# A transformer block: gates and part of the first inner layer as fills, and steps of the attention loop ordered in twos

## The reference, cut to what matters

```python
def _mole(x, W, b, A, Bm, Rw):
    gates = jax.nn.softmax(jnp.einsum('bsd,de->bse', x, Rw), axis=-1)
    base = jnp.einsum('bsd,dh->bsh', x, W) + b
    z = jnp.einsum('bsd,edr->ebsr', x, A)
    zg = z * jnp.transpose(gates, (2, 0, 1))[..., None]
    return base + SCALING * jnp.einsum('ebsr,erh->bsh', zg, Bm)

h = _layernorm(x) * (1 + ca) + sa
x = x + ga * attention(h, W_qkv, b_qkv, W_out, b_out)
h = _layernorm(x) * (1 + cb) + sb
h = relu(_mole(h, W1, b1, A1, B1, R1))
x = x + gb * _mole(h, W2, b2, A2, B2, R2)
```

## Time and profile before

| what | us |
|---|---|
| median of 3 executions (lowest, highest) | 1315.23 (1310.58, 1323.12) |
| the profiled execution | 1316.99 |
| its span, first to last instruction | 1315.0 |
| PE busy | 1222.3 |
| DVE busy | 934.4 |
| ACT busy | 800.2 |
| POOL busy | 183.3 |

### The profile page before, as it was taken

One profiled execution on the slowest core, in us unless ns is written; L12 is line 12 of the kernel. 1 busy time (PEld: TensorE's weight loads), 2 busy tenths in 40 slices (PEclk: granted clock), 3 DMA queues, 4 the chain that ended last, 5 costly groups with the idle time before them and its releaser, 6 DMA issues.

```text
span 1315.0 us, 23664 instructions
## 1 busy us (share of the span) xinstructions
PE 1222.3 (93%) x9456; PEld 709.5 (54%) x9456; DVE 934.4 (71%) x1247; ACT 800.2 (61%) x1611; POOL 183.3 (14%) x153
## 2 busy tenths in 40 slices
PE   7988789999999999999999999999989999999997
PEld 6765333444444344444444444334334888888886
DVE  4877897888787888777888778776531477776653
ACT  4441466777667777767777767776664455454442
POOL 5205600000112000000000000201010133232310
PEclk9997799999999999999999989999787999999998
DMA  5793120031142022022022013400000122211100
GB/s 169 245 289 140 51 64 10 16 83 29 35 107 60 9 64 54 10 62 71 10 54 56 10 32 102 113 1 9 11 10 22 45 64 65 54 50 38 53 17 33
DMA packets 58118, 79.53 MB, mean 60 GB/s; under 512 B 12680, under 2 KB 28752, under 8 KB 58008
## 3 DMA queue, kind: packets, MB, share of 16 engines
q1 hardware_dynamic: 58008, 78.01, 20.3%
HBM read 47.57 MB, written 29.62 MB: 59 GB/s over the span
## 4 chain that ended last, share of the span: by engine, by line
PE 68%; DVE 17%; ACT 8%; issue 4%; SPq 2%; DMA 2%; ACTq 0%; DVEq 0%
PE ps L893 21%; PE ps L875 17%; PE ps L855 9%; PE ps L965 7%; PE ps L391 6%; ACT prob L1074 6%; PE ps L811 6%; DVE mx L1222 5%; DVE hid_lo L1365 4%; DVE xhat L419 1%; DVE stats L409 1%; SPq L453 1%; DMA xs<-in_x 1%; ACT o_sb L1059 1%; DVE x L1270 1%
## 5 line engine op out<-in xcount | busy, mean ns | idle before, releaser
L1074 ACT ACTIVATE prob<-ps 128x512 f32<-128x512 f32 (+3 forms) x1280 | 597.8, 536 | 267.9 <-PE ps L811 137.9
L1222 DVE TENSOR_REDUCE mx<-ps 128x2 f32<-128x1024 f32 (+1 forms) x512 | 591.5, 1187 | 164.1 <-PE ps L855 92.9
L875 PE MATMUL ps<-qst,kst 64*128 64x512 f32 (+3 forms) x1280 | 379.5, 450 | 14.9 <-ACT prob L1074 9.1
L875 PEld LDWEIGHTS ps<-qst,kst 64*128 64x128 f32 x1280 | 174.8, 188 | 325.9 <-ACT prob L1074 284.0
L893 PE MATMUL ps<-prob,vw 128*32 128x512 f32 (+3 forms) x2560 | 309.6, 557 | 9.2 <-ACT o_sb L1059 9.1
L855 PE MATMUL ps<-kst,qst 62*128 62x512 f32 (+3 forms) x1280 | 248.8, 419 | 23.3 <-DVE mx L1222 19.1
L855 PEld LDWEIGHTS ps<-kst,qst 62*128 62x128 f32 x1280 | 125.9, 193 | 68.6 <-DVE mx L1222 58.8
L811 PE MATMUL ps<-mask_kh,eye_h 64*128 64x128 bf16 x1024 | 100.8, 227 | 0.0
L893 PEld LDWEIGHTS ps<-prob,vw 128*32 128x32 f32 x2560 | 51.9, 109 | 74.9 <-ACT prob L1074 49.8
L1365 DVE TENSOR_TENSOR hid_lo<-hidf,hid_hi 128x512 fp32r<-128x512 f32 x64 | 73.1, 1182 | 13.8 <-ACT hid_hi L1114 13.7
L1218 DVE TENSOR_REDUCE mx<-ps 128x4 f32<-128x512 f32 x64 | 59.8, 954 | 21.1 <-PE ps L811 21.1
(11 more groups left out here) (157 smaller groups left out, 1358.0 us busy)
## 6 DMA issues: line engine op xcount, KB each, us to landing
qk_parts<-parts SPq DMA_DIRECT2D x32, 512.0 KB, 4.9
qst<-qk_parts SPq DMA_DIRECT2D x192, 64.0 KB, 2.4
kst<-qk_parts SPq DMA_DIRECT2D x192, 64.0 KB, 2.4
xs<-in_x SPq DMA_DIRECT2D x16, 512.0 KB, 8.4
o_all<-o_sb SPq DMA_DIRECT2D x32, 256.0 KB
o_raw<-o_all SPq DMA_DIRECT2D x16, 256.0 KB
rd<-rden_rows SPq DMA_DIRECT2D x16, 256.0 KB
out<-y SPq DMA_DIRECT2D x8, 512.0 KB, 3.2
```

The source lines that it names most:

```text
L875: last = pe.matmul(ps[:, banks[par], 0:BLK - skip], kst[g % 2][rows, pair, t * P:(t + 1) * P], qst[g % 2][rows, pair, J * BLK + skip:(J + ...
L1074: act.activation(prob[:, n % P_BUFS, h, 0:width], ps[:, L_BANK + i % L_BUFS, 0:width], ACT.Exp).then_inc(exp_done, 1)
L1222: dve.tensor_reduce(mx[:, u % 2, :, pairs[0], r, cb], ps[:, bank:bank + 2, 0:width], AX, ALU.max).then_inc(max_red, 1)
```

## The change

**Order of the steps.** Steps are taken in twos. A pair whose steps are off the diagonal, which is not the first pair of its unit, and which has at most four pieces of fills, goes a new way: values products come later, the first of them in two halves of its columns, and head 3 of the first step is paired with head 0 of the second. Other pairs keep the former order. Long fills are made in pieces (`pieces_of`): the projection and the routing in four, the turn and a hidden chunk in two.

**More of block 0 among the fills.** The front events get fixed steps: projection 285, scaling 290, turn 292, routing 295, weighing 297, gates 299, hidden chunks 0 to 3 at 302, 306, 310 and 314 (before, the projection was at 287, the turn at 302). They are inserted after the planner has placed the others. The maxima around them move by a step or two. ACT reads a hidden chunk in the step after it, in two halves behind heads 1 and 3. Chunks 4 and 5 stand before the last two values products. Then come the projection of block 1, chunks 6 and 7, and block 0's down products.

**Other places.** POOL casts and splits block 1's attention output behind the projection. The gate rows are computed after the first block's projections to q and k. The arrays of the last stage lie elsewhere: hidden chunk 2 of block 0 is in `o_raw` of even blocks, chunk 3 in `rd` of even blocks, and the load of block 2 has a wait for `z2_done`.

```diff
+EARLY_H = 4
+FRONT = [(285, ("project", 0)), (290, ("rescale", 0)), (292, ("turn_x", 0)), (295, ("route", 0)), (297, ("weigh", 0)),
+         (299, ("gates", 0))] + [(302 + 4 * m, ("hidden", m)) for m in range(EARLY_H)]
...
+ROOT_FRONT, GATE_FRONT = SLOT_OF[FRONT_FILL["project", 0]] + 3, SLOT_OF[FRONT_FILL["route", 0]] + 1
+def pieces_of(es):
+    parts = {"project": TT, "route": TT, "turn_x": KC, "hidden": KC}
+    return [(e, k) for e in es for k in range(parts.get(EVENTS[FILLS[e]][0], 1))]
...
+        for m, at in ((2, o_raw_at), (3, rd_at)):
+            hid_front.append(Region(at).pair(f"hid_{m}", [P, BLK]))
...
                 def load(i):
                     until(sp, o_lo, i - 1)
+                    if i == 2:
+                        sp.wait_ge(z2_done, 1)
...
-                load(2)
                 for q in range(2):
                     sp.wait_ge(o_stored[q], 16 * O_DMAS * NU // 2)
                     sp.wait_ge(rden_stored[q], 16 * NG // 2)
+                load(2)
...
                 normalise_o(1)
+                pool.wait_ge(o_norm, 2)
+                pool.wait_ge(fill_done, FRONT_FILL["project", 0] + 1)
+                pool.tensor_copy(oT[0][:], o_raw[1][:]).then_inc(o_hi, 1)
+                pool.wait_ge(o_hi, 2)
+                pool.tensor_tensor(oT[1][:], o_raw[1][:], oT[0][:].bitcast(F32), ALU.subtract).then_inc(o_lo, 1)
...
-                pe.wait_ge(setup, 2 * KC)
-                gate_rows()
                 pe.wait_ge(w_lo, 2)
                 project_qk(0, range(0, KC))
                 turn(1)
                 project_qk(0, range(KC, 2 * KC))
+                pe.wait_ge(setup, 2 * KC)
+                gate_rows()
...
+                    if ev[0] == "hidden":
+                        m = ev[1]
+                        pe.wait_ge(max_red, FRONT_FILL["gates", 0] + 1)
+                        pe.wait_ge(ffn_lo, 2 * W_PIECES)
+                        product(pe, ps[:, bank, :], lambda v, c: w1_p[v][:, k, m * P:(m + 1) * P],
+                                lambda v, c: hT2[0][v][:, k, :], 1, start=(k == 0), stop=False)
+                        if k == KC - 1:
+                            pe.matmul(ps[:, bank, :], bl1_s[:, m * P:(m + 1) * P], zgT_front[:],
+                                      start=False, stop=True).then_inc(fill_done, 1)
...
-                for n in range(NS):
-                    if n >= PV_LAG:
-                        values(n - PV_LAG)
-                    logits(n, 0)
-                    for e in ORDER[1 + n][:2]:
-                        fill(e)
-                    logits(n, 1)
-                    for e in ORDER[1 + n][2:]:
-                        fill(e)
-                for n in range(NS - PV_LAG, NS):
-                    values(n)
+                for n in range(0, NS, 2):
+                    each = [pieces_of(ORDER[1 + n]), pieces_of(ORDER[2 + n])]
+                    both = each[0] + each[1]
+                    u = STEPS[n][0]
+                    if not diagonal(n) and n > FIRST[u] and len(both) <= 4:
+                        logits((n, 0), (n, 1))
+                        for piece in both[0:1]:
+                            fill(*piece)
+                        logits((n, 2))
+                        values(n - 2, 0)
+                        logits((n, 3), (n + 1, 0))
+                        for piece in both[1:2]:
+                            fill(*piece)
+                        values(n - 2, 1)
+                        logits((n + 1, 1))
+                        for piece in both[2:3]:
+                            fill(*piece)
+                        logits((n + 1, 2), (n + 1, 3))
+                        values(n - 1)
+                        for piece in both[3:]:
+                            fill(*piece)
+                    else:
+                        for m in (n, n + 1):
+                            mine = each[m - n]
+                            cut = 1 if m + 1 in HIDDEN_STEP else 2
+                            if m >= PV_LAG:
+                                values(m - PV_LAG)
+                            logits((m, 0), (m, 1))
+                            for piece in mine[:cut]:
+                                fill(*piece)
+                            logits((m, 2), (m, 3))
+                            for piece in mine[cut:]:
+                                fill(*piece)
+                hidden_front(EARLY_H)
+                values(NS - 2)
+                hidden_front(EARLY_H + 1)
+                values(NS - 1)
...
-                pe.wait_ge(small_lo, 4)
-                pe.wait_ge(ffn_lo, 2 * W_PIECES)
-                route_in(0)
+                project_out(1)
+                for m in range(EARLY_H + 2, FC):
+                    hidden(0, m)
+                    hidden_low_rank(0, m)
...
+                def early_hidden_out(m, part):
+                    e = FRONT_FILL["hidden", m]
+                    act.wait_ge(fill_done, e + 1)
+                    if part == 0:
+                        if m >= 2:
+                            act.wait_ge(max_red, FRONT_FILL["hidden", m - 2] + 1)
+                        if m == 0:
+                            act.wait_ge(pv_done, LAST_OF_G[NG - 2] + 1)
+                    dst = hidf_front[:, m % 2, :] if part == 0 else hid_at(0, m, 0)
+                    act.activation(dst, ps[:, S_BANK + 2 * (e % 2), :], ACT.Relu,
+                                   bias=b1_sb[:, m:m + 1]).then_inc(f1_out, 1)
...
-                exponentials(0, z1_sub, z1_exp)
                 for i in range(NBLK):
                     if i >= 1:
-                        exponentials(i - 1, z2_sub, z2_exp)
-                    if i + 1 < NBLK:
+                        exponentials(i - 1, z2_sub, z2_exp, 1)
+                    if 1 <= i < NBLK - 1:
                         o_high(i + 1)
-                    gated_in(i)
-                    for m in range(FC):
+                    if i >= 1:
+                        gated_in(i)
+                    for m in range(0 if i >= 1 else EARLY_H, FC):
                         hidden_out(i, m)
```

More of the change, by code:

```diff
@@ L860, in fill, with routed, hidden_front, logits @@
                         for at in range(len(pairs)):
-                            last = mask((bank, bank + 1), (at + 1) * width - P, mask_qh)
+                            last = mask_queries(bank, (at + 1) * width - P)
                     last.then_inc(fill_done, 1)
-                def logits(n, pair):
+                def routed(i, bank, t):
+                    return product(pe, ps[:, bank, t * 32:t * 32 + ZP],
+                                   lambda v, k: hT2[i % 2][v][:, k, t * P:(t + 1) * P],
+                                   lambda v, k: ar1_p[v][:, k, :], KC)
+                def hidden_front(m):
+                    pe.wait_ge(max_red, NF)
+                    product(pe, ps[:, H_BANK + m % 2, :], lambda v, k: w1_p[v][:, k, m * P:(m + 1) * P],
+                            lambda v, k: hT2[0][v][:, k, :], KC, stop=False)
+                    pe.matmul(ps[:, H_BANK + m % 2, :], bl1_s[:, m * P:(m + 1) * P], zgT_front[:],
+                              start=False, stop=True).then_inc(f1_done, 1)
+                def logits(*heads):
+                    for n, h in heads:
+                        u, t = STEPS[n]
+                        g, J = UNITS[u]
+                        skip = skip_of(n)
+                        if n == FIRST[u] and h == 0:
+                            pe.wait_ge(m_in[u % 2], 16 * M_DMAS * (u // 2 + 1))
+                        until(pe, exp_done, 4 * n + h - L_BUFS + 1)
+                        rows = slice(h % 2 * STACK, h % 2 * STACK + ROWS + MROWS)
+                        last = pe.matmul(ps[:, L_BANK + (4 * n + h) % L_BUFS, 0:BLK - skip],
+                                         kst[g % 2][rows, h // 2, t * P:(t + 1) * P],
+                                         qst[g % 2][rows, h // 2, J * BLK + skip:(J + 1) * BLK],
+                                         start=True, stop=True)
+                        if not diagonal(n):
+                            last.then_inc(st_done, 1)
+                    if diagonal(heads[0][0]):
+                        mask_keys(heads)
+                def values(n, part=None):
                     u, t = STEPS[n]
@@ L1043, in _ @@
                 root(1)
-                act.wait_ge(rows_done, 1)
-                for v in range(2):
-                    act.copy(gates[:, v].rearrange("p b d -> p (b d)"), ps[:, V_BANK + v, :]).then_inc(rows_out, 1)
                 act.wait_ge(setup, 2 * KC + 1)
@@ L1393, in _ @@
                         gate_y(i - 1)
-                    if front:
+                    if front and back:
                         low_o(i + 1)
```

320 lines of the change are left out of this document (203 added, 117 removed).

## The result

| | us |
|---|---|
| before, median of 4 (lowest, highest) | 1316.43 (1310.58, 1323.12) |
| after, median of 4 (lowest, highest) | 1339.16 (1333.98, 1343.97) |
| ratio, 95% interval | 1.0178 (1.0139 to 1.0218) |
| the profiled execution after, its span | 1343.97, 1341.8 |

What follows compares the result with a forecast made beforehand. Attention was taken as paced by a loop of latencies between PE and ACT, PE the bound from block 1 on; -20 + 10 + 4 - 15 + 11 - 3 = -13 from 1317.0 gave 1304, as median 1302 us; range 1285 to 1322.

Steps and rivals of the forecast that it cites:

- Part 1: Attention steps in the two-step order: 57 pairs save 28 us, 26 runs cost 8; net -20 us, bounds -38 and +8.
- Rival 4: Slower: values products at run ends cost 1.0 us each, pairs save nothing; +8 instead of -20, 1330 us; chance 0.06.
- Rival 1: Two-step order gives little: fills waiting for DVE hold logits, 0.2 us a pair, -8 instead of -20; 1314 us; chance 0.20.
- Rival 5: Clock: the 11 us wait is followed by 13.6 us at 1.2 GHz; +7 and none of the -3, 1312 us; chance 0.10.
- Part 2: Last attention group: routing, pieces and four hidden chunks among the fills cost +10 us, bounds 2 and 16.
- Parts 3 and 4: Chunks 4 and 5 before the last values products, +4 us; block 0 after the last unit's copy, -15 us.
- Part 5: Start of block 1: block 2's load waits for block 0's down products; +11 us, from 0 to 16.
- Part 6: First stage: gate rows behind the first projections start ACT and DVE earlier; -3 us, bounds 0 and -6.
- The clock: PE's granted clock: chunks fill some gaps (-3 us), the load's wait makes a new one (+3); zero in sum.

Runs made afterwards that it cites:

- no_chunks: two_chunks with no hidden chunk among the fills: chunks 0 and 1 before the last values products, the others behind; 1316.29 us, 1.0014 of the kernel before.
- two_chunks: Changed kernel with only hidden chunks 0 and 1 as fills, 2 and 3 in the tail, block 2's load without its wait; 1315.14 us, ratio 1.0018.
- other_array: Changed kernel with hidden chunks 2 and 3 in the arrays of odd blocks, so block 2's load needs no wait; 1321.83 us, 1.0057 of before.
- no_pairs: Changed kernel with every pair of steps in the former order; 1335.52 us, 1.0161 of the kernel before.
- gate_rows_later: Kernel before with only the gate rows moved behind the first block's projections; 1318.24 us, 1.0031 of the kernel before.
- whole_values: two_chunks with a pair's first values product whole, where its first half stood; 1336.95 us, 1.0175 of the kernel before.

## Why the prediction was wrong

The direction was wrong, and the sum: -13 forecast; between the means of the runs it is +23.8 (1315.25 to 1339.07), of which +15.6 is work at equal clock and +8.2 clock. By its own parts:

| part | forecast | measured |
|---|---|---|
| 1 two-step order | -20 | -1 to +1 |
| 2 front in the last group | +10 | +19 |
| 3 tail | +4 | +3.1 |
| 4 block 0 after the copy | -15 | -13.7 |
| 5 load of block 2 | +11 | +13.0 |
| 6 gate rows | -3 | 0 |
| clock | 0 | +8 |

The measured column does not add up to +23.8, mainly because rows 4 and 5 are differences between two profiles and hold clock (some -2 and +5 us) that the last row counts again. Free of clock, the stretches add up to +15.6, as the last column of the table of stretches shows.

**Part 1 failed, and it is the largest miss.** The hand-written pair of 4.89 us came out at 5.09; the schedule was right up to the last values product (3.42 forecast, 3.51 in the rows), and the fill behind it held the next logits for 0.34 instead of 0.24. That alone would have left 0.24 a pair. The other half of the failure: the sum priced all 47 pairs with four fills by the one drawn with full products. In 15 of the 25 inner ones fills lie on the diagonal, their mask products go through PE, and the pair became 0.2 to 0.4 longer than before instead of 0.44 shorter. The pairs with fewer fills fell short too: 0.18 saved with three (0.68 forecast), 0.57 with two (0.9). The evidence was in the profile of before: a group of 1024 mask products on the queries' side, which no step of the forecast counted:

```profile
L811 PE MATMUL ps<-mask_qh,eye_h 64*128 64x128 bf16 x1024 | 66.1, 225 | 0.0
```

Rival 4 named this (pairs that save nothing, run ends that cost) and gave it 0.06, though with a cost of 8 us that is not there; it ought to have had more, since the sum rested on one class of pair drawn. Rival 1's number does not follow from its own words: 57 pairs at 0.2 less the 8 for the runs save 3, not 8, which gives 1319 instead of 1314. The order's true place is beyond it, at nothing. Rival 5 counts the stretch behind the wait twice, as the +3 of the sum and again as +7.

**Part 2 was mis-sized**, beyond its upper bound of 16. A hidden chunk costs 1.64 us on PE and two ACT operations of 0.58, together 2.8. The forecast let half of ACT's part vanish in its idle time and took 1.7 a chunk. Measured: 5.7 and 6.1 us for two chunks each (no_chunks, two_chunks, other_array), 2.95 a chunk, or 2.65 at equal clock, so next to nothing was hidden. In this loop of latencies, idle time of an engine was not room: a product put into PE's order delays the next logits, and an operation put into ACT's delays the bank. The rest, routing and pieces, was put at 3.2 and is +11.0, or 8 if the 8 us more at 1.2 GHz are taken off at 0.37. Together 19 (15 with the former order of steps, from 108.6 to no_pairs' 124.1). Why routing, gates and pieces cost two to three times their price was not tried, and this cause stays open.

**Parts 3 and 4 were right** (+3.1 as the copy's lag behind the last exponential, 1.1 to 4.2; -13.7; the last low part comes 14.0 us after the copy's start, 15 forecast). Only, part 2 costs more than part 4 gains.

**Part 5 was right** in mechanism and nearly in size: POOL at 10.8 us after Z (10.1), the cast done 14.2 after it (14.4). The lost time is 12.1 at ACT's first chunk. What it had wrong is the clock around it, put at +3 and taken back by a -3 that did not come.

**Part 6 failed too**, by 3 us: the gain of ACT and DVE did not reach the stage's end (gate_rows_later).

**The clock** was put at zero, and rival 5 at 0.10 with +7. It is +8.2 in the means, of which some 3 are time in which PE was waiting anyway. Part of it is the stretch seen above: 1.2 GHz from inside the wait until 1087. The chunks did not fill the gaps of the last group, for which the forecast took 3 us off: 34.1 us at 1.2 GHz there, 32.4 before. The Trainium skill ("TensorE: Matmul & The Clock Gate", section "HAM oscillation") says that a product stream interrupted by a long wait restarts cold; the rows of 1072 to 1087 agree, with a clock of 0.51 behind the wait. Part of it is elsewhere: in blocks 2 to 6 of the kernel after the clock falls once a block for 3.4 us, which makes a block 37.4 instead of 35.9. That comes and goes between kernels: two_chunks has it in one block, the kernel before in some, no_chunks in nearly all and other_array in all, both without the wait. It cannot be put down to the wait by these runs; what sets it stays open.

## What to carry to other kernels

An array that is reused to save space is a dependence: other_array is the same work with two arrays placed one slot further on, and it takes back 16 of the 23 us (9 of the 15.6 at equal clock). Ask of every added wait what is queued behind the data it delays, and put the reuse where the space is already free. And before moving work "under" a loop, ask what paces the loop: where two engines wait on each other, neither's idle time takes work for nothing, and a gain from reordering has to be worked out for each kind of step in it, not for the plainest.

## What the runs showed of the hardware

- The time of this kernel follows the mean granted clock of the execution, 0.99 us for 0.001, and that clock ranged from 0.949 to 0.970 in the kernel before alone: 20 us between its lowest and its highest time. Two profiles can differ by 10 us in one stage by that alone (the last group, 120.6 and 110.6 for the same instructions), so differences between single profiles need the clock column beside them. A microsecond at 1.2 GHz costs this kernel 0.37 to 0.39 us by three measures: the last group, the slope over whole executions, and a single pair of steps (6.46 instead of 5.14 with 3.4 us of it).
- Going from products on row halves to the values' column tiles shows as idle time of the weight load with nothing to wait for: 0.37 us at 441.92 and 0.36 at 444.87, before two of the three parts of the values product (before the third the profile names a wait for ACT). Going back shows 0.84 us before the fill at 445.87. The Trainium skill states in "TensorEngine Tiling (Array Packing)", section "Key Properties", that a change of tiling mode drains the array, and the rows fit that; a pair in the new order makes three such changes and back where two steps of before make two. I did not weigh it in the forecast. The halving still pays (whole_values), so it is no reason against it here.
